# Two rings of PSUM banks in the first layer's attention: from four and three banks to five and two

## The chip, the cores and the metric

The kernel runs on one core of one Trainium2 chip. Five engines work side by side: TensorE (PE) multiplies and writes PSUM alone, VectorE (DVE) and ScalarE (ACT) read PSUM, GpSimd (POOL) works in SBUF, and SyncE (SP) issues transfers. PSUM has eight banks of 128 x 512 float32 here. The metric is the time of one execution in microseconds (us) on the device, the median of several runs.

## The reference, cut to what matters

Two layers over a batch of eight sequences of 512 tokens with 128 channels. The change lies in the attention of the first layer (`L0`): 16 heads of 8 channels, keys within 256 positions of the query.

```python
q, k, v = (proj(w, b) for w, b in ((wq, bq), (wk, bk), (wv, bv)))   # 16 heads of 8
...
scores = jnp.einsum('bhncd,bhnkd->bhnck', qb, kb) / scale
...
scores = jnp.where(valid[None, None], scores, -jnp.inf)
p = jax.nn.softmax(scores, axis=-1)
o = jnp.einsum('bhnck,bhnkd->bhncd', p, vb)
o = o.reshape(B, H, T, D).transpose(0, 2, 1, 3).reshape(B, T, E)
return o @ wo + bo
```

Behind it come a mixture of experts on the same normalised input and the whole second layer, which the change does not touch.

## The kernel before

The first layer's attention takes about the first 525 us. It runs once per sequence (`b`), as a "body" of 64 steps written out one by one: `start` and `first` for sequence 0, six bodies of kind `loop`, then `last`, and `finish`, which holds only the tail of sequence 7. The 64 steps are 4 groups of heads (g) x 4 tiles of 128 queries x 4 heads. Every engine walks through the same steps in this fixed order, and semaphores alone hold one engine back for another; no scheduler moves anything.

Scores are computed twice. In step n PE's `score_rows(n)` multiplies queries by keys into one bank ("rows", 384 or 512 columns), and DVE's `maximum` (L1510) reads it and finds each query's largest score. From the maxima of a group `max_rows` makes `q_max` (L1524). Then `score_cols` computes the scores transposed, with the maximum taken off ("cols"), 21 steps later than the rows of the same number, and ACT's `exp_of` (L1238) writes their exponentials to SBUF. POOL masks them (L1012). Every fourth step ends with `values`, four matmuls of exponentials by values (two passes each, x8 in the trace), into the bank `gather_a`, which belongs to no ring.

So a step of PE is: rows(n), sometimes one thing more, cols(n-21), sometimes one thing more, and in steps with n % 4 = 1 `values`. The things more, per group of 16 steps (n mod 16): at 2 `turn_max` (transposes for `q_max`), at 3 and 7 `select("k")` and `select("q")` of a later group of heads, at 12 `turn_out` (transposes of `o_raw`, which ACT copies out of `gather_a` at L1246). Once per body: `project_v` at step 26, `turn_heads` at 32, `project_out` ("attended") at 36, `turn_x` at 40, `project_raw` at 43 and 45, and the router's logits at 47.

Two rings of banks lie between PE and its readers. A `Fills` object numbers what is filled in the order of the program, puts fill m into slot m modulo the ring's length, and has PE wait, before fill m, until fill m minus the length has been read (`fillable`). Ring M (PE to DVE) takes rows, the transposes of `turn_max`, `turn_out`, `turn_heads`, v, logits and attended: 76 fills in a loop body, in four banks: the three `ring_d` and `gather`. Ring A (PE to ACT) takes cols, `select`, `turn_x` and `project_raw`: 75 fills in a loop body, in three banks: both halves of `ring_a0` and the first half of `ring_a1`. The other half of `ring_a1` is `gather_a`. In the trace, PE's matmuls have the line L458 (L462 for transposes), that of the helper which issues them, and tiles lose their numbers: `ring_a<-q_max,rows` is a cols, `ring_a<-halves,sel` a select, `ring_d<-rows,q_rows` or `gather<-rows,q_rows` a rows, `ring_a<-arena,v_aug` a values.

PE's instructions are issued in order: one that waits for a bank holds up all that stand behind it.

Of the kernel before, what the change touches and what calls it, by code (L numbers as in the profile page):

```python
# [26 lines left out]
B = 8  # L27
T = 512
# [77 lines left out]
class Signal:  # L106


    def __init__(self, ctx, nc, phase, name, per):
        self.name = f"{phase}_{name}"  # L110
        self.sem = ctx.enter_context(nc.semaphore(self.name))
        self.most = 0
        self.per, self.credit, self.n = per, CREDITED.get(name, 0), 0
# [16 lines left out]
class Count:  # L130
# [6 lines left out]
    def open(self, kind, b):  # L137

        assert self.n in (0, self.total), (self.name, kind, self.n, self.total)
        start, first, loop, last, _ = (self.totals[k] for k in BODIES)  # L140
        done = start + first
        self.step, self.known = (b, done - loop) if kind == "loop" else (None, {
            "start": 0, "first": start, "last": done + (B - 2) * loop, "finish": done + (B - 2) * loop + last}[kind])
        self.total, self.n = self.totals[kind], 0
        self.first_fill = {"start": 0, "first": start, "loop": done, "last": done + (B - 2) * loop,
                           "finish": done + (B - 2) * loop + last}[kind]

    def add(self, k):
# [28 lines left out]
class Fills:  # L177


    def __init__(self, body, full, free, slots):  # L180
        self.body, self.full, self.free, self.slots = body, full, free, slots
        self.numbers = {k: {} for k in BODIES}
        assert full.totals["loop"] % len(slots) == 0

    def of(self, what):

# [20 lines left out]
def at_least(eng, count, value):  # L207

    if not isinstance(value, int) or value > 0:
        eng.wait_ge(count.sem, value)  # L210
# [31 lines left out]
def two_layers(nc, x, wq, bq, wk, bk, wv, bv, wo, bo, w_router, w1, b1, w2, b2,  # L242
# [4 lines left out]
    with ExitStack() as ctx:  # L247
        def sb(name, shape, dt=F32):
            return ctx.enter_context(nc.sbuf_tensor(name, shape, dt))
# [5 lines left out]
        banks_d = [ctx.enter_context(nc.psum_tensor(f"ring_d{n}", [P, T], F32)) for n in range(DR)]  # L255
        gather = ctx.enter_context(nc.psum_tensor("gather", [P, T], F32))
        banks_a = [ctx.enter_context(nc.psum_tensor(f"ring_a{n}", [P, 2 * T], F32)) for n in range(AR)]
# [32 lines left out]
        slots, slots_now = sb("slots", [P, TT], U32), sb("slots_now", [P, NT], U32)  # L290
# [8 lines left out]
        full, hi = fulls[:, 0, :], halves[:, 0, :]  # L299
# [95 lines left out]
        def signals(phase, per):  # L395
# [8 lines left out]
            s["D"] = Ring(s["d_full"], s["d_free"], banks_d)  # L404
            s["A"] = Ring(s["a_full"], s["a_free"], banks_a)
            return s

        SA = {name: Count(ctx, nc, name, totals) for name, totals in PER_A.items()}
        now = Body(list(SA.values()))
        M = Fills(now, SA["m_full"], SA["m_free"], [bank[:] for bank in banks_d] + [gather[:]])  # L410
        A = Fills(now, SA["a_full"], SA["a_free"], [banks_a[0][:, 0:T], banks_a[0][:, T:2 * T], banks_a[1][:, 0:T]])
        gather_a = banks_a[1][:, T:2 * T]
        k_dma = [sem(f"k_padded{g}") for g in range(G)]

# [39 lines left out]
        def _(pe):  # L454
            pe.wait_ge(s_pool, N_POOL)

            def mm(out, lhs, rhs, start=True, stop=True):
                return pe.matmul(out, lhs, rhs, start=start, stop=stop, skip_group_check=True)  # L458

            def turn(slot, tile_of, n=NT):  # L460

                return [pe.transpose(slot[:, i * P:(i + 1) * P], tile_of(i), ident[:]) for i in range(n)][-1]  # L462
# [4 lines left out]
            def turn_x():  # L467

                at_least(pe, SA["xn"], SA["xn"].at(1))
                at_least(pe, A.free, A.fillable("xn.T"))  # L470
                turn(A.slot("xn.T"), lambda i: xn[:, i, :]).then_inc(A.full.sem, A.full.add(1))

            def project_raw(which):

                at_least(pe, A.free, A.emptied("xn.T"))
                at_least(pe, A.free, A.fillable(("raw", which)))
                mm(A.slot(("raw", which)), w_nat[:, "kq".index(which), :], xn_t[:]).then_inc(A.full.sem, A.full.add(1))

# [11 lines left out]
            def project_v():  # L490

                at_least(pe, M.free, M.fillable("v"))
                [mm(M.slot("v")[:, i * P:(i + 1) * P], xn_t[:, i * P:(i + 1) * P], wv_sb[:])
                 for i in range(NT)][-1].then_inc(M.full.sem, M.full.add(1))

            def route():

                at_least(pe, M.free, M.fillable("logits"))
                [mm(M.slot("logits")[:, i * NE:(i + 1) * NE], xn_t[:, i * P:(i + 1) * P], router_sb[:])
                 for i in range(NT)][-1].then_inc(M.full.sem, M.full.add(1))  # L500

# [1465 lines left out]
```

## Time and profile before

| what | us |
|---|---|
| median of three runs (1407.49 to 1410.2) | 1408.0 |
| the profiled execution | 1407.57 |
| its span, first to last instruction | 1405.6 |
| PE busy in the span | 1227.9 |
| DVE busy | 902.2 |
| ACT busy | 680.2 |
| POOL busy | 455.8 |
| length of the stage that the change touches, about | 525 |

The profiled execution's own time is 2.0 us above its span; what is added to the span is added to the time. The granted PE clock, in tenths of full speed, is given for slices or stretches of the span.

### The profile page before, as it was taken

How to read it: one execution, taken by the hardware profiler on the slowest of the kernel's cores; microseconds unless marked ns; L12 is line 12 of the kernel's file. 1: busy time of each engine (PE TensorE's matmuls, PEld its weight loads, DVE VectorE, ACT ScalarE, POOL GpSimd, SP SyncE). 2: the span in 40 equal slices, each digit the busy share in tenths (PEclk: the TensorE clock that was granted, in tenths of full speed). 3: DMA queues.
4: the chain of work that ended last, by engine and by line, in shares of the span. 5: the costliest groups of instructions: out<-in, count | busy, mean ns of one | idle time of the engine just before them, and what ended most of it. 6: DMA issues, size and time to landing. Idle time of an engine off the chain costs nothing.

```text
span 1405.6 us, 27026 instructions
## 1 busy us (share of the span) xinstructions
PE 1227.9 (87%) x8812; PEld 844.3 (60%) x8812; DVE 902.2 (64%) x2473; ACT 680.2 (48%) x1293; POOL 455.8 (32%) x694
## 2 busy tenths in 40 slices
PE   3699999999999984999379899898998989989896
PEld 2455556555555543999355656656665576655664
DVE  5788878788888846444345665647565566655744
ACT  1366666766666651444154353553526445254450
POOL 2122212222221216432135253442525335253330
PEclk9899999999999995999679999999999999999999
DMA  2400100100000006112000000000000000000000
GB/s 57 95 17 16 24 16 16 24 16 20 20 16 16 23 2 202 49 45 41 15 5 5 3 12 0 11 4 7 7 0 15 0 7 7 0 15 0 8 2 8
DMA packets 34597, 29.78 MB, mean 21 GB/s; under 512 B 5984, under 2 KB 27104, under 8 KB 34528
## 3 DMA queue, kind: packets, MB, share of 16 engines
q1 hardware_dynamic: 32224, 24.22, 6.5%
q0 software_dynamic: 2304, 4.72, 1.5%
q8 instruction: 34, 0.56, 0.2%
q14 instruction: 35, 0.29, 0.1%
HBM read 13.72 MB, written 6.82 MB: 15 GB/s over the span
## 4 chain that ended last, share of the span: by engine, by line
PE 33%; issue 9%; ACT 5%; DVE 2%; POOL 2%; POOLq 0%; ACTq 0%; DVEq 0%
PE ring_a L458 12%; PE ring_d L458 11%; PE gather L458 7%; ACT arena L1382 3%; PE ring_a L462 2%; ACT xn_all L1362 1%; POOL q_len L1147 1%; DVE arena L1888 0%; POOL klen L1153 0%; DVE k_rows L1816 0%; ACT arena L1354 0%; ACT k_rows L1321 0%; DVE m_cols L1874 0%; POOL arena L1171 0%; DVE q_rn L1752 0%
## 5 line engine op out<-in xcount | busy, mean ns | idle before, releaser
L1238 ACT ACTIVATE arena<-ring_a 128x384 f32<-128x384 f32 (+1 forms) x512 | 255.2, 549 | 152.0 <-PE ring_a L458 152.0
L1382 ACT ACTIVATE arena<-ring_a 128x896 f32<-128x896 f32 (+1 forms) x192 | 163.3, 885 | 205.4 <-PE ring_a L458 205.4
L1510 DVE CUSTOM_DVE_ANT_0 arena<-ring_d,arena 128x384 bf16<-128x384 f32 (+1 forms) x377 | 226.6, 619 | 45.1 <-PE ring_d L458 39.6
L458 PE MATMUL ring_a<-rows,k_rows 64*128 64x512 f32 (+3 forms) x1536 | 159.3, 341 | 43.8 <-ACT xn_all L1362 26.4
L458 PE MATMUL ring_a<-q_max,rows 128*128 128x384 f32 (+1 forms) x512 | 194.5, 383 | 1.0 <-ACT arena L1238 0.5
L1012 POOL TENSOR_SCALAR_AFFINE_SELECT arena<-arena 128x512 f32<-128x512 f32 x128 | 81.9, 640 | 349.5 <-ACT arena L1238 349.5
L458 PEld LDWEIGHTS ring_a<-rows,k_rows 64*128 64x128 f32 x1536 | 119.9, 191 | 81.2 <-ACT xn_all L1362 29.3
L458 PE MATMUL ring_d<-rows,q_rows 128*128 128x384 f32 (+1 forms) x377 | 152.7, 407 | 14.3 <-DMA rows<-k_rows 13.7
L1147 POOL TENSOR_TENSOR q_len<-q_sum,exponents 128x8 f32<-128x8 f32 x64 | 105.2, 1643 | 180.4 <-DVE q_sum L1792 180.4
L458 PE MATMUL ring_d<-arena,v_aug 128*64 128x512 f32 (+3 forms) x1024 | 150.2, 438 | 0.0
L458 PEld LDWEIGHTS ring_d<-rows,q_rows 128*128 128x128 f32 x377 | 72.0, 191 | 92.1 <-DVE mx L1510 43.8
L458 PE MATMUL ring_a<-arena,v_aug 128*32 128x384 f32 (+1 forms) x1024 | 122.8, 551 | 1.0 <-POOL arena L1012 1.0
L458 PEld LDWEIGHTS ring_d<-arena,v_aug 128*64 128x64 f32 x1024 | 68.0, 136 | 78.9 <-issue 68.9
L1171 POOL TENSOR_SCALAR_AFFINE_SELECT arena<-arena 128x256 f32<-128x256 f32 x256 | 97.3, 409 | 42.9 <-ACT arena L1382 42.9
L1792 DVE TENSOR_REDUCE q_sum<-arena 128x8 f32<-128x512 f32 x64 | 43.8, 684 | 100.7 <-ACT arena L1354 100.7
L1510 DVE CUSTOM_DVE_ANT_0 arena<-gather,arena 128x512 bf16<-128x512 f32 (+1 forms) x135 | 84.4, 625 | 34.9 <-PE gather L458 30.0
L458 PEld LDWEIGHTS ring_a<-q_max,rows 128*128 128x128 f32 x512 | 96.0, 188 | 16.5 <-ACT arena L1238 4.5
L1294 ACT ACTIVATE arena<-ring_a,arena 128x128 f32<-128x128 f32 x160 | 50.0, 364 | 75.2 <-PE ring_a L458 75.2
L1846 DVE COPY arena<-ring_d 128x512 f32<-128x512 f32 x64 | 43.8, 685 | 64.8 <-PE ring_d L458 64.8
L1810 DVE TENSOR_TENSOR rows<-arena,rows 128x512 fp32r<-128x512 f32 x64 | 44.6, 697 | 61.9 <-ACT rows L1370 61.0
L458 PE MATMUL ring_a<-arena 128*128 128x128 f32 x320 | 78.1, 399 | 0.0
L458 PEld LDWEIGHTS ring_a<-arena 128*128 128x128 f32 x320 | 76.2, 328 | 0.1
(217 smaller groups left out, 2053.0 us busy)
## 6 DMA issues: line engine op xcount, KB each, us to landing
rows<-k_rows SPq DMA_DIRECT2D x128, 64.0 KB, 2.0
arena<-in_w SPq DMA_DIRECT2D x2, 2048.0 KB, 14.5
slots_y<-arena SPq DMA_DIRECT2D x40, 64.0 KB, 1.6
x_all<-in_x SPq DMA_DIRECT2D x8, 256.0 KB, 4.4
tokens_x<-xn_all SPq DMA_DIRECT2D x1, 2048.0 KB, 9.6
out<-o_t SPq DMA_DIRECT2D x8, 256.0 KB, 2.3
arena<-tokens_x,tokens_now POOLq DMA_INDIRECT x40, 2.6
wq_sb<-in_wq_t SPq DMA_DIRECT2D x1, 512.0 KB, 6.6
```

The source lines that it names most:

```text
L458: return pe.matmul(out, lhs, rhs, start=start, stop=stop, skip_group_check=True)
L462: return [pe.transpose(slot[:, i * P:(i + 1) * P], tile_of(i), ident[:]) for i in range(n)][-1]
L1012: pool.affine_select(out=v, in_=v, compare_op=ALU.is_ge, fill=0.0, base=0, pattern=[[0, HG], [1 if late else -1, P]], channel_multiplier=- ...
L1147: pool.tensor_tensor(q_len[:, 0:2 * NT], q_sum[:, 0:2 * NT], exponents[:, NT:3 * NT], ALU.pow).then_inc(s["lens"].sem, s["lens"].add(1))
L1171: ins = pool.affine_select(out=v, in_=v, compare_op=ALU.is_ge, fill=0.0, base=0, pattern=[[0, 2], [1, P]], channel_multiplier=-1)
L1238: act.activation(probs[:, t % NT, h, 0:many], A.slot(("cols", c))[:, 0:many], ACT.Exp).then_inc(A.free.sem, A.free.add(1))
L1294: ins = act.activation(hidden[:, u % 2, c], hidden_bank(u, c), ACT.Relu, bias=staged[:, u, AT_B1 + c:AT_B1 + c + 1])
L1382: act.activation(dst, src, ACT.Exp).then_inc(A.free.sem, A.free.add(1))
L1510: dve.tensor_tensor_reduce(dump[:, h % 2, 0:many], M.slot(("max", n))[:, 0:many], masks[:, m, at:at + many], 1.0, LOWEST, ALU.add, ALU.max ...
L1792: dve.reduce_sum(q_sum[:, 0:2 * NT], q_sq, AX.X).then_inc(s["sums"].sem, s["sums"].add(1))
L1810: dve.tensor_tensor(q_lo[:, n % QB, :], q_full, q_hi[:, n % QB, :].bitcast(F32), ALU.subtract).then_inc(s["q_lo"].sem, s["q_lo"].add(1))
L1846: dve.tensor_copy(o1[:, n, :], D.slot(("o", n))[:]).then_inc(D.free.sem, D.free.add(1))
```

## The change

One bank, the first half of `ring_a1`, moves from ring A to ring M. Ring A has two places instead of three, ring M five instead of four. Since 76 and 75 are not multiples of 5 and 2, the number of the first fill of a loop body now depends on the body, and the assertion that the rings divide the counts goes. No instruction that computes is added, removed or put elsewhere in the order; banks and the numbers that PE waits for change.

```diff
@@ -142,7 +142,7 @@
         self.total, self.n = self.totals[kind], 0
-        self.first_fill = {"start": 0, "first": start, "loop": done, "last": done + (B - 2) * loop,
+        self.first_fill = {"start": 0, "first": start, "loop": done + (b - 1) * loop, "last": done + (B - 2) * loop,
                            "finish": done + (B - 2) * loop + last}[kind]
@@ -180,7 +180,6 @@
         self.numbers = {k: {} for k in BODIES}
-        assert full.totals["loop"] % len(slots) == 0
@@ -407,8 +406,8 @@
-        M = Fills(now, SA["m_full"], SA["m_free"], [bank[:] for bank in banks_d] + [gather[:]])
-        A = Fills(now, SA["a_full"], SA["a_free"], [banks_a[0][:, 0:T], banks_a[0][:, T:2 * T], banks_a[1][:, 0:T]])
+        M = Fills(now, SA["m_full"], SA["m_free"], [bank[:] for bank in banks_d] + [gather[:], banks_a[1][:, 0:T]])
+        A = Fills(now, SA["a_full"], SA["a_free"], [banks_a[0][:, 0:T], banks_a[0][:, T:2 * T]])
```

Two places on PE, each in the same loop body. The first is steps 2 to 5 of a group, from `turn_max` on: cols, rows, cols, select k, rows, cols, rows, cols, values. The names are out<-in with bank numbers; `ring_a0` stands for either of its two halves; `A_a_free` counts what ACT has read. Before:

```order
L462 MATMUL gather<-ident,m_cols 128x128 x3
L458 MATMUL ring_a0<-q_max,rows 128x384 [waits A_a_free]
L458 MATMUL ring_d0<-rows,q_rows 128x384 [waits A_m_free]
L458 MATMUL ring_a1<-q_max,rows 128x384 [waits A_a_free]
L458 MATMUL ring_a0<-halves,sel 128x512 [waits A_a_free]
L458 MATMUL ring_a0<-halves,sel 128x512
L458 MATMUL ring_d1<-rows,q_rows 128x512 [waits A_m_free]
L458 MATMUL ring_a0<-q_max,rows 128x384 [waits A_a_free]
L458 MATMUL ring_d2<-rows,q_rows 128x512 [waits A_m_free]
L458 MATMUL ring_a1<-q_max,rows 128x512 [waits A_a_free,A_m_free]
L458 MATMUL ring_a1<-arena,v_aug 32x384 [waits A_masked]
```

And now:

```order
L461 MATMUL ring_d2<-ident,m_cols 128x128 x3
L457 MATMUL ring_a0<-q_max,rows 128x384 [waits A_a_free]
L457 MATMUL gather<-rows,q_rows 128x384 [waits A_m_free]
L457 MATMUL ring_a0<-q_max,rows 128x384 [waits A_a_free]
L457 MATMUL ring_a0<-halves,sel 128x512 [waits A_a_free]
L457 MATMUL ring_a0<-halves,sel 128x512
L457 MATMUL ring_a1<-rows,q_rows 128x512 [waits A_m_free]
L457 MATMUL ring_a0<-q_max,rows 128x384 [waits A_a_free]
L457 MATMUL ring_d0<-rows,q_rows 128x512 [waits A_m_free]
L457 MATMUL ring_a0<-q_max,rows 128x512 [waits A_a_free,A_m_free]
L457 MATMUL ring_a1<-arena,v_aug 32x384 [waits A_masked]
```

The order is the same. All five fills of ring A now share the two halves of `ring_a0`: the select takes the bank of the cols two fills before it, and the last cols that of the select. `ring_a1` takes a rows.

The second place is steps 6 to 9 of the same group, around select q. Before:

```order
L458 MATMUL gather<-rows,q_rows 128x512 [waits A_m_free]
L458 MATMUL ring_a0<-q_max,rows 128x512 [waits A_a_free]
L458 MATMUL ring_d0<-rows,q_rows 128x512 [waits A_m_free]
L458 MATMUL ring_a0<-q_max,rows 128x512 [waits A_a_free]
L458 MATMUL ring_a1<-halves,sel 128x512 [waits A_a_free]
L458 MATMUL ring_a1<-halves,sel 128x512
L458 MATMUL ring_d1<-rows,q_rows 128x512 [waits A_m_free]
```

And now:

```order
L457 MATMUL ring_d1<-rows,q_rows 128x512 [waits A_m_free]
L457 MATMUL ring_a0<-q_max,rows 128x512 [waits A_a_free]
L457 MATMUL ring_d2<-rows,q_rows 128x512 [waits A_m_free]
L457 MATMUL ring_a0<-q_max,rows 128x512 [waits A_a_free]
L457 MATMUL ring_a0<-halves,sel 128x512 [waits A_a_free]
L457 MATMUL ring_a0<-halves,sel 128x512
L457 MATMUL gather<-rows,q_rows 128x512 [waits A_m_free]
```

Here too only banks differ: the select moved from `ring_a1` to the bank of the cols that stands two fills before it.

## Rows read from the trace of the kernel before

**Rows 1.** The page: span, and busy time of PE and its weight loads.

```profile
span 1405.6 us, 27026 instructions
PE 1227.9 (87%) x8812; PEld 844.3 (60%) x8812; DVE 902.2 (64%) x2473; ACT 680.2 (48%) x1293; POOL 455.8 (32%) x694
```

**Rows 2.** Busy time, in three stretches: PE, PEld, DVE, ACT, POOL, then granted clock, DMA share, GB/s.

```profile
100.00:450.00 350.00, 334.32 (x1984) 203.27 (x1984) 288.96 (x1010) 232.40 (x479) 77.87 (x117) 1.00 0.08 18
...
530.00:560.00 30.00, 11.89 (x44) 10.00 (x45) 19.96 (x43) 2.38 (x5) 22.64 (x46) 0.50 0.77 236
...
900.00:1000.00 100.00, 91.61 (x796) 62.00 (x796) 61.54 (x130) 45.87 (x71) 46.22 (x66) 1.00 0.03 7
```

**Rows 3.** Groups by line and shape, 100 to 450 us: exponentials, both widths.

```profile
L1238 ACT ACTIVATE arena<-ring_a 128x512 f32<-128x512 f32 x188 | 109.1, 606 | 48.9 <-PE ring_a L458 48.9
...
L1238 ACT ACTIVATE arena<-ring_a 128x384 f32<-128x384 f32 x185 | 82.7, 492 | 65.6 <-PE ring_a L458 65.6
```

**Rows 4.** Waits, 100 to 450 us: total us, times, longest us.

```profile
PEld ring_d L458 <- DVE mx L1510: 30.9, 48, 0.8
...
PEld ring_d L462 <- ACT o_raw L1246: 18.0, 24, 0.9
...
PEld ring_a L458 <- ACT halves L1211: 4.1, 6, 0.7
...
PEld ring_a L458 <- DVE q_max L1524: 2.3, 6, 0.4
```

**Rows 5.** Timeline, one group of 16 steps, 270.81 to 284.20 us.

```profile
271.47 1.64 ACT L1238 ACTIVATE arena<-ring_a 128x384 f32<-128x384 f32 x4 [0.92 <-PE ring_a L458]
...
271.62 0.19 PEld L458 LDWEIGHTS ring_a<-q_max,rows 128*128 128x128 f32 x1
...
272.01 0.19 PEld L458 LDWEIGHTS ring_a<-q_max,rows 128*128 128x128 f32 x1
...
272.41 1.06 PE L458 MATMUL ring_a<-arena,v_aug 128*32 128x512 f32 x8
...
273.41 0.19 PEld L458 LDWEIGHTS ring_d<-rows,q_rows 128*128 128x128 f32 x1 [0.84 <-DVE mx L1510]
...
274.48 0.36 PEld L458 LDWEIGHTS ring_a<-halves,sel 128*128 128x128 f32 x2
274.50 0.87 ACT L1238 ACTIVATE arena<-ring_a 128x384 f32<-128x384 f32 x2 [1.39 <-PE ring_a L458]
...
274.65 0.62 PE L458 MATMUL ring_a<-halves,sel 128*128 128x512 f32 x2
...
275.32 0.69 ACT L1220 ACTIVATE k_rows<-ring_a,ones_row 128x512 fp32r<-128x512 f32 x1
...
275.52 0.19 PEld L458 LDWEIGHTS ring_a<-q_max,rows 128*128 128x128 f32 x1
...
276.07 0.85 PE L458 MATMUL ring_a<-arena,v_aug 128*32 128x384 f32 x8
...
276.86 0.19 PEld L458 LDWEIGHTS gather<-rows,q_rows 128*128 128x128 f32 x1 [0.62 <-DVE mx L1510]
...
277.62 1.09 ACT L1238 ACTIVATE arena<-ring_a 128x512 f32<-128x512 f32 x2 [0.75 <-PE ring_a L458]
...
277.66 0.42 PEld L458 LDWEIGHTS ring_a<-halves,sel 128*128 128x128 f32 x2
...
278.59 0.61 ACT L1222 ACTIVATE q_rows<-ring_a 128x512 fp32r<-128x512 f32 x1
...
278.81 0.19 PEld L458 LDWEIGHTS ring_a<-q_max,rows 128*128 128x128 f32 x1
...
279.35 0.16 PEld L458 LDWEIGHTS ring_a<-arena,v_aug 128*32 128x32 f32 x8 [0.35 <-issue]
...
282.04 0.42 PEld L462 LDWEIGHTS ring_d<-ident,o_raw 128*128 128x128 f32 x4 [0.92 <-ACT o_raw L1246]
...
284.20 0.19 PEld L458 LDWEIGHTS ring_d<-rows,q_rows 128*128 128x128 f32 x1 [0.84 <-DVE mx L1510]
```

## The prediction

> **What bounds the kernel now.** I first read the page: PE is busy 1227.9 of 1405.6 us, DVE 902.2 and ACT 680.2 [rows 1]. That is a mean over stages, so I cut out the stage of the change. From 100 to 450 us PE is busy 334.32 of 350 us, DVE 288.96, ACT 232.40, and the clock is granted in full, 1.00 [rows 2]. A row of PE is to be read with care, because its matmuls overlap, so I then asked what PE waits for. The table of waits names DVE first: 30.9 us over 48 waits [rows 4]. It would follow that ring M is too short. The timeline says otherwise. The weight load of the rows behind a `values` always stands 0.84 us "behind DVE" when the values had 512 columns and 0.62 us when they had 384 [rows 5]; 30.9/48 is 0.64, a mixture of just these. The load comes 1.00 us after the values' matmuls began (272.41 to 273.41) or 0.79 us (276.07 to 276.86), never at another distance. That is the length of the values' own streaming, 1.06 and 0.85 us busy with the drain in it; DVE merely happened to be the last to have signalled. PE works there. The real waits of PE are few: for `o_raw`, 18.0 us over 24 times; for the second raw projection, 4.1 over 6; for `q_max`, 2.3 over 6 [rows 4].
>
> So PE, in order, sets the pace, and it waits neither for DVE nor, but for the six, for ACT. What a loop body costs: cols are 188 + 185 = 373 in 350 us [rows 3], 0.938 us a step, 60.0 us for 64 steps.
>
> **Ring M, four to five.** What a fifth bank can take away is a wait of PE for DVE to read a rows. After the correction above no such wait of weight is left, and I price this part at 0. Bound on the side of a gain: if all of the 30.9 us in 350 were true, then over some 480 us of bodies 30.9/350 x 480 = 42 us. I take 0, because the gaps have the two fixed lengths of the streaming, not lengths that vary with DVE. A rule reads such rows the other way: the Trainium skill, "Perfetto Trace Analysis", section "Optimization Strategy", says that a gap which repeats on the engine that should be saturated can mean too few PSUM buffers. By it the repeated gap would be worth up to those 42 us; by the row it is worth nothing. A bank's new reader costs nothing: DVE reads as many columns as before.
>
> **Ring A, three to two.** Now fill m waits for the reading of fill m-2 and not m-3. I re-time one plain group [rows 5], 270.81 to 284.20 us. I need two small figures. With three banks the fourth of four narrow cols had just to wait for the first: the four exponentials start at 271.47 and one takes 0.492 us [rows 3], which ends at 271.96, and the load came at 272.01. So from the end of the reading to PE's weight load 0.05 us pass. And a load normally leads its matmul (274.48 to 274.65, 0.17 us), while after a wait the lead is shorter; I take the matmul's delay as the load's less 0.1 us.
>
> - *Four narrow cols (steps 14 to 1).* The third one's load stood at 271.62; it must now wait for the first exponential, to 272.01: +0.39. The four exponentials take 1.64 us, so the second ends (1.64 - 0.49)/3 = 0.38 us after the first, at 272.34, and the fourth load comes at 272.39 instead of 272.01: +0.38, not additive. All that follows is 0.38 us later.
> - *Around select k (steps 2 to 5).* Its load (274.48) waits for the first exponential (274.50 + 0.49 = 274.99), to 275.04: +0.56; matmuls +0.46. Its matmuls ended at 275.27 and now at 275.73; ACT's copy of 0.69 us, which began at 275.32, begins at 275.78 and ends at 276.47. The last cols needs that bank: 276.52 instead of 275.52, +1.00, less 0.1: +0.90.
> - *Around select q (steps 6 to 9).* The first exponential ends 277.62 + 0.61 = 278.23; the select's load moves from 277.66 to 278.28, matmuls +0.52; the copy from 278.59 to 279.11, ending at 279.72; the last cols' load from 278.81 to 279.77, +0.96, less 0.1: +0.86.
> - *Steps 10 to 13.* 0: here `turn_out` waits 0.92 us for `o_raw` anyway, and no cols stands within two fills of an unread one. That wait is no reserve for the others, since `o_raw` hangs on the values before it and moves with them.
>
> A group: 0.38 + 0.90 + 0.86 = 2.14 us; four: 8.6. Of that three things go once per body. The `q_max` wait (2.3/6 = 0.4) already holds the last cols of one group: -0.4. `turn_heads` stands between narrow cols and gives ACT the time: -0.4. `project_out` stands between select k and the last cols, likewise, and has a wait for DVE of its own: -0.9. Three more fills of ring A enter, x transposed and two raw projections, each read by ACT in 0.6 to 1.3 us; one of them waits 0.7 us already [rows 4]. I take +0.75, an estimate between 0 and three times the 0.56 of a select (1.7). Sum: 8.6 - 1.7 + 0.75 = 7.6 us per loop body (rounded), 60.0 to 67.6.
>
> Behind PE everything shifts as a whole: ACT's and DVE's work per body is unchanged, and both had waited for PE (48.9 + 65.6 us before the exponentials alone [rows 3]).
>
> All bodies: six loop bodies 45.6. `first` has cols in 43 of 64 steps: 43/64 x 7.6 = 5.1. `last` has no next sequence, so no raw projections and no selects of group 0: 5. `finish` has 21 cols, mostly held by ACT already: 1.5. Sum 57.2 us. On the profiled execution's 1407.57 us that is **1465 us**; its median of three, 1408.0, lies 0.4 us higher, which is inside the rounding.
>
> **Rivals.**
>
> - *The fifth bank pays (faster).* The mechanism is the table of waits taken at its word: PE does wait for DVE's maximum before the rows that follow values. Place: the 48 waits; price: up to -42 us, 1366 us before what ring A costs. It decides if ring A's waits come to under 42 us. For it: the table and ACT's busy share of 232.40 in 350. Against: the two fixed lengths. Chance 4%.
> - *Nothing moves.* ACT is a third idle, and the waits at ring A fall into places where PE would have waited for something else. Then 1408 us. For it only the means speak; in the re-timed group all but one of the places have no other wait. Chance 3%.
> - *Half the price.* The waits for `o_raw`, 24 of 0.75 us, are after all a reserve (if ACT takes its exponentials earlier relative to values). 2.14 - 0.75 = 1.39 a group, 5.6 for four, less 1.7 plus 0.75 gives 4.6 per body; counted as 7.5 bodies (57.2/7.6) 35 us: 1442 us. Chance 15%.
> - *Nothing is absorbed.* 8.6 + 1.7 = 10.3 us per body, 77 us in all: 1485 us. Chance 13%.
> - *The clock falls.* Where PE was busy only 11.89 of 30 us its granted clock was 0.50, the lower of the two levels; at 91.61 of 100 us it was 1.00 [rows 2]. After the change PE would be busy about 57 of 67.6 us, 85%, nearer to the second. If it fell for a tenth of PE's time, that tenth would take twice as long: 5.7 us per body, 43 in all on top: 1508 us. Chance 4%. The Trainium skill, "TensorE: Matmul & The Clock Gate", section "A second HAM failure mode: psum-queue depth-cycling", tells of a kernel in which short idles between groups, from cycling through PSUM banks, made the clock swing; no stretch of this trace with PE over nine tenths busy shows that.
>
> **How the numbers follow.** The forecast itself, within 1450 to 1479, has 61%. The range reaches down to the half price, 1440, and up to the case without absorption, 1485, and leaves out the rest. A measurement of this kernel tells 0.2%, about 3 us, from no change. Slower by more: 0.61 + 0.15 + 0.13 + 0.04 = 0.93; same 0.03; faster 0.04.
>
> **What would show it.** In the profile after: (1) a row "PEld ring_a <- ACT arena L1237" among the longest waits, some 12 per body, where none stands now, and "<- ACT k_rows" and "q_rows" before the last cols of two stretches per group; (2) the gaps of 0.84 and 0.62 us behind `values` as before, whether named DVE or "issue", which proves the first paragraph; (3) 67 to 68 us per body; (4) DVE waiting longer for PE; (5) clock 1.00 in the stage; (6) nothing different behind it. The prediction is wrong if the gaps behind values shrink, if ACT's copies of the selects come no later against the loads, or if PE's rows can be seen issued past a waiting cols.

## The result and the profile after

The changed kernel takes 1469.64 us (median of four runs, 1466.49 to 1471.78) against 1407.74 us before: 1.0436 times as long, 95% interval 1.0408 to 1.0463. Forecast were 1465 us, 1440 to 1485. The profiled execution took 1467.64 us, 60.1 more than the 1407.57 of before; the sum had said 57.2.

The page of the changed kernel: span, busy times, and the granted clock in 40 slices of the span.

```profile
span 1465.7 us, 27027 instructions
...
PE 1268.2 (87%) x8812; PEld 841.3 (57%) x8812; DVE 902.1 (62%) x2473; ACT 696.0 (47%) x1293; POOL 457.0 (31%) x694
...
PEclk9899999999999999599958999999999999999998
```

DVE's work is the same to 0.1 us. PE "works" 40.3 us more though it runs the same 8812 matmuls. Their records overlap: where nothing waits, a narrow matmul's record lasts 0.34 us and the next begins 0.17 us after it (271.27 and 271.44 in the trace of before). When the next one is held up, more of the record before it counts as busy, and the one behind the wait is itself about 0.1 us longer, 0.44 us at 297.70 in the rows below. How the 40.3 us divide between the two was not worked out. The share of busy time, 87%, has not moved at all, which shows how little it tells about a kernel that got 4% slower.

Where the time lies is told by the issue of the transfer `tokens_x`, the first thing behind the stage. Before and after:

```profile
L922 SPq DMA_DIRECT2D tokens_x<-xn_all x1: 391/391/391, 529.2 to 529.2; - x1
```

```profile
L921 SPq DMA_DIRECT2D tokens_x<-xn_all x1: 392/392/392, 587.4 to 587.4; - x1
```

587.4 - 529.2 = 58.2 us of the 60.1 stand in the first layer's attention.

Busy time and clock of the changed kernel from 100 to 450 us (PE, PEld, DVE, ACT, POOL, clock), which answers to the first of [rows 2], and the waits of the same stretch, which answer to [rows 4]:

```profile
100.00:450.00 350.00, 321.89 (x1758) 176.36 (x1754) 255.55 (x892) 216.50 (x425) 69.54 (x105) 1.00 0.07 17
```

```profile
PEld ring_a L457 <- ACT arena L1237: 30.8, 62, 0.7
PEld ring_d L457 <- DVE mx L1509: 30.7, 42, 0.8
...
PEld gather L457 <- DVE mx L1509: 11.7, 16, 0.8
PEld ring_a L457 <- DVE mx L1509: 11.5, 16, 0.8
...
PEld ring_a L457 <- ACT q_rows L1221: 6.8, 16, 0.4
...
PE ring_a L457 <- ACT k_rows L1219: 3.5, 15, 0.2
```

The first row is new: 62 waits of PE for an exponential, where [rows 4] had none. The rows that name DVE are still there, now split over the bank names `ring_d`, `gather` and `ring_a`, because rows rotate through five banks: 42 + 16 + 16 = 74 waits of at most 0.8 us. Before, they were 71 and not 48, since the table of before has a second row of this kind, for `gather`. It has a third row with DVE in it, a short one, in which matmuls stand still and not only weight loads:

```profile
PEld gather L458 <- DVE mx L1510: 17.2, 23, 0.9
...
PE gather L458 <- DVE mx L1510: 3.5, 6, 0.6
```

This last row, once per body, has no counterpart in the changed kernel. It is the one wait that the fifth bank did take away, as the section on the experiments shows; the gaps behind `values` it did not touch. The clock stayed at 1.00, its upper level.

The order of the weight loads in a plain group of 16 steps, with ACT's instructions that hold them up (start, length, engine; the idle time before each in brackets). It answers to [rows 5]:

```profile
296.50 0.19 PEld L457 LDWEIGHTS gather<-rows,q_rows 128*128 128x128 f32 x1 [0.84 <-DVE mx L1509]
...
297.16 1.90 ACT L1237 ACTIVATE arena<-ring_a 128x384 f32<-128x384 f32 x4 [0.92 <-PE ring_a L457]
297.70 0.19 PEld L457 LDWEIGHTS ring_a<-q_max,rows 128*128 128x128 f32 x1 [0.36 <-ACT arena L1237]
297.70 0.44 PE L457 MATMUL ring_a<-q_max,rows 128*128 128x384 f32 x1
...
298.46 1.06 PE L457 MATMUL ring_a<-arena,v_aug 128*32 128x512 f32 x8
...
300.55 0.87 ACT L1237 ACTIVATE arena<-ring_a 128x384 f32<-128x384 f32 x2 [1.49 <-PE ring_a L457]
301.09 0.30 PEld L457 LDWEIGHTS ring_a<-halves,sel 128*128 128x128 f32 x2 [0.55 <-ACT arena L1237]
...
301.85 0.69 ACT L1219 ACTIVATE k_rows<-ring_a,ones_row 128x512 fp32r<-128x512 f32 x1 [0.43 <-PE ring_a L457]
...
302.65 0.19 PEld L457 LDWEIGHTS ring_a<-q_max,rows 128*128 128x128 f32 x1 [0.58 <-issue]
...
303.08 0.85 PE L457 MATMUL ring_a<-arena,v_aug 128*32 128x384 f32 x8
...
305.27 0.30 PEld L457 LDWEIGHTS ring_a<-halves,sel 128*128 128x128 f32 x2 [0.66 <-ACT arena L1237]
...
306.70 0.19 PEld L457 LDWEIGHTS ring_a<-q_max,rows 128*128 128x128 f32 x1 [0.43 <-ACT q_rows L1221]
...
307.13 0.85 PE L457 MATMUL ring_a<-arena,v_aug 128*32 128x384 f32 x8
...
309.82 0.42 PEld L461 LDWEIGHTS ring_a<-ident,o_raw 128*128 128x128 f32 x4 [0.92 <-ACT o_raw L1245]
...
311.99 0.19 PEld L457 LDWEIGHTS ring_d<-rows,q_rows 128*128 128x128 f32 x1 [0.84 <-DVE mx L1509]
```

Each stretch runs from one `values` to the next (the first and last from the rows behind one):

| stretch | before | after | more | forecast |
|---|---|---|---|---|
| four narrow cols | 270.81 to 272.41: 1.60 | 296.50 to 298.46: 1.96 | 0.36 | 0.38 |
| around select k | 272.41 to 276.07: 3.66 | 298.46 to 303.08: 4.62 | 0.96 | 0.90 |
| around select q | 276.07 to 279.35: 3.28 | 303.08 to 307.13: 4.05 | 0.77 | 0.86 |
| steps 10 to 13 | 279.35 to 284.20: 4.85 | 307.13 to 311.99: 4.86 | 0.01 | 0 |
| group | 13.39 | 15.49 | 2.10 | 2.14 |

The load at 302.65 shows how to read a releaser: it says "issue" (elsewhere DVE), but k_rows ends at 301.85 + 0.69 = 302.54 and its matmul's own row says `[0.23 <-ACT k_rows L1219]`. It is the select's bank that the cols waits for.

### The profile page after: what moved, and what is told of

It is laid out like the page before. It is cut to its first block, busy times and chain, and to the rows that moved or that the text cites. A ratio compares the mean times of both kernels' runs of the same rounds, so it can differ in the third digit from the quotient of the medians.

```text
span 1465.7 us, 27027 instructions
## 1 busy us (share of the span) xinstructions
PE 1268.2 (87%) x8812; PEld 841.3 (57%) x8812; DVE 902.1 (62%) x2473; ACT 696.0 (47%) x1293; POOL 457.0 (31%) x694
## 4 chain that ended last, share of the span: by engine, by line
PE 69%; issue 12%; ACT 11%; POOL 3%; DVE 3%; SPq 1%; DMA 1%; POOLq 0%; ACTq 0%; DVEq 0%
PE ring_a L457 38%; PE ring_d L457 17%; PE gather L457 9%; ACT arena L1237 3%; PE ring_a L461 3%; ACT arena L1381 3%; PE ring_d L461 1%; ACT xn_all L1361 1%; ACT k_rows L1219 1%; ACT o_raw L1245 1%; POOL v_aug L1040 1%; POOL q_len L1146 1%; PE gather L461 1%; DVE rows L1585 0%; SPq L876 0%
## 5 line engine op out<-in xcount | busy, mean ns | idle before, releaser
L1237 ACT ACTIVATE arena<-ring_a 128x384 f32<-128x384 f32 (+1 forms) x512 | 263.7, 542 | 170.5 <-PE ring_a L457 164.4
L1509 DVE CUSTOM_DVE_ANT_0 arena<-ring_d,arena 128x384 bf16<-128x384 f32 (+1 forms) x312 | 187.5, 621 | 86.8 <-PE ring_d L457 84.5
L457 PE MATMUL ring_a<-q_max,rows 128*128 128x384 f32 (+1 forms) x512 | 205.5, 403 | 11.6 <-ACT k_rows L1219 5.2
L457 PE MATMUL ring_d<-rows,q_rows 128*128 128x384 f32 (+1 forms) x312 | 125.0, 403 | 12.7 <-DMA rows<-k_rows 12.4
L457 PEld LDWEIGHTS ring_d<-rows,q_rows 128*128 128x128 f32 x312 | 59.7, 192 | 74.3 <-DVE mx L1509 48.0
L1509 DVE CUSTOM_DVE_ANT_0 arena<-gather,arena 128x512 bf16<-128x512 f32 (+1 forms) x100 | 62.1, 621 | 25.9 <-PE gather L457 25.3
L457 PE MATMUL gather<-wout_sb,arena 128*128 128x128 f32 x512 | 68.8, 281 | 8.7 <-DVE arena L1887 8.7
```

Of the source, the lines that this page charges most:

```text
L1237: act.activation(probs[:, t % NT, h, 0:many], A.slot(("cols", c))[:, 0:many], ACT.Exp).then_inc(A.free.sem, A.free.add(1))
L1509: dve.tensor_tensor_reduce(dump[:, h % 2, 0:many], M.slot(("max", n))[:, 0:many], masks[:, m, at:at + many], 1.0, LOWEST, ALU.add, ALU.max ...
```

## The experiments

Each is compared with the kernel before, run on the same chip. `e1` to `e3` change the lists of banks alone, `e4` also gives the selects a ring with semaphores of its own. Beside the time of the whole kernel stands the length of a loop body, from one router projection to the next in the kernel's trace. Within a trace the six loop bodies mostly agree to 0.03 us, so it can tell what the times of whole executions, which scatter by several us, cannot. It is the length in one execution of each kernel: 59.9 us before (one body 60.15), 67.8 in the changed kernel.

**e1: only ring A's loss.**

```diff
-        M = Fills(..., [bank[:] for bank in banks_d] + [gather[:], banks_a[1][:, 0:T]])
+        M = Fills(..., [bank[:] for bank in banks_d] + [gather[:]])
```

> Ring A two banks as in the change, ring M four as before; the eighth bank is used by nobody. Theory (only ring A's lost bank costs, ring M was never short): the time of the changed kernel, 1466 to 1473 us. Rival (the fifth bank of ring M earns part of the 42 us that the table of waits offers, and ring A costs more than is seen): slower than the changed kernel by over 3 us, 1473 to 1510 us.

Measured: 1470.02 us, ratio 1.044 (1.0412 to 1.0469). The changed kernel's own ratio is 1.0436. Taking the fifth bank away again costs nothing that these intervals, some 4 us wide to each side, can tell, and a bank worth 42 us is excluded.

The traces are finer, and there ring M was short in one place. The six loop bodies of e1 take 68.3 to 68.4 us, those of the changed kernel 67.8. All of the difference, 0.53 us, lies in the one stretch between two `values` that holds `project_out`: 5.56 us in e1, 5.03 with the fifth bank; every other stretch agrees to 0.02 us. The kernel before shows why:

```profile
239.94 0.34 PE L458 MATMUL gather<-rows,q_rows 128*128 128x384 f32 x1
...
242.50 0.55 DVE L1510 CUSTOM_DVE_ANT_0 arena<-gather,arena 128x384 bf16<-128x384 f32 x1
...
242.98 0.08 DVE L1510 DVE_READ_ACCUMULATOR2_ANT mx<- 128x1 f32 x1
...
243.21 0.57 PE L458 MATMUL gather<-arena,o_t 128*128 128x128 f32 x3 [0.59 <-DVE mx L1510]
```

The bank `gather` is filled by a rows. Four fills later `attended` wants the same bank, but DVE, which has meanwhile copied `o_t` and normalised x, reads the rows only from 242.50 to 243.06. So PE stands still for 0.59 us: the bank's old content had not yet been read. In e1 the same wait is 0.3 us (5 times in 350 us), and in the changed kernel `attended` follows the matmul before it with no wait. Over some 7.5 bodies the fifth bank is worth about 4 us: a tenth of the rival's 42, but not the 0 of the theory.

**e2: ring M with three, ring A with three.**

```diff
+        M = Fills(..., [bank[:] for bank in banks_d[:2]] + [gather[:]])
+        A = Fills(..., [banks_a[0][:, 0:T], banks_a[0][:, T:2 * T], banks_a[1][:, 0:T]])
```

> Ring A three banks as before, ring M three; one bank unused. Theory (with four banks PE never waits for DVE): with three, by the group of rows 5, the fourth narrow rows waits for the maximum three before it, some 0.4 us per group and a little more where DVE has other work: 2 to 3 us per body, 1420 to 1430 us. Rival (the waits for DVE behind values are true): each of the eight or so per body grows by one maximum, 0.55 to 0.7 us, at least 5 us per body: 1445 us or more.

Measured: 1419.27 us, ratio 1.0077 (1.005 to 1.0104), 11 to 12 us more than before, just below the range that was said (1420 to 1430) and far from the rival's 1445. A body takes 61.5 us, 1.5 more than before, where 2 to 3 were expected. The table of waits of this kernel (100 to 450 us):

```profile
PEld ring_d L457 <- DVE mx L1509: 46.1, 80, 0.8
PEld gather L457 <- DVE mx L1509: 22.4, 39, 0.8
```

119 waits against 71 before, in which true short ones are now mixed with the streaming, and with gaps that the table of before put down to "issue" or to other instructions of DVE. At three banks the ring bites in most groups: the stretch with the narrow cols is 0.24 us longer. At four it bites once per body, at `attended`.

**e3: the change turned round, four for ring A, three for ring M.**

```diff
+        M = Fills(..., [bank[:] for bank in banks_d[:2]] + [gather[:]])
+        A = Fills(..., [banks_a[0][:, 0:T], banks_a[0][:, T:2 * T], banks_a[1][:, 0:T], banks_d[2][:]])
```

> The change turned round: ring A four banks, ring M three. Theory: ring A was short only at the second raw projection (0.7 us per body) and by 0.05 us at the fourth narrow cols, so this is 5 to 8 us below the kernel with three and three, 1413 to 1424 us, and not faster than before. Rival (any bank given to ring A pays as much as the one taken from it cost): 1350 to 1400 us.

Measured: 1413.79 us, ratio 1.0044 (1.0029 to 1.0058). 5.5 us below the kernel with three and three and still above before, as expected. The two intervals overlap a little, but no run of either kernel falls among those of the other, and a body takes 60.8 us instead of 61.5, nearly all of it in the stretch with the second raw projection (4.81 instead of 5.45 us). So for ring A the third bank is worth 62 us, and a fourth one, beside three for ring M, 5.5.

**e4: the selects in a bank of their own.** Ring A has two banks, ring M four, and the eighth bank is a ring S of length one, with its own semaphores.

```diff
+        S = Fills(now, SA["s_full"], SA["s_free"], [banks_a[1][:, 0:T]])
...
-                at_least(pe, A.free, A.fillable(("sel", which, g)))
+                at_least(pe, S.free, S.fillable(("sel", which, g)))
```

> Ring A two banks, but the two select fills of a group go to the eighth bank, a ring of one of their own; ring M four. Theory (most of the cost is the select, which waits for an exponential and whose copy holds the bank of the last cols): 0.90 and 0.86 us of each group go, 0.38 for narrow cols and about 0.75 per body for raw projections and the transposed x stay: 1.9 us per body, 1422 us, 1417 to 1430. Rival (two banks are too few for the cols and their exponentials as such): over 1445 us.

Measured: 1426.37 us, ratio 1.0143 (1.0097 to 1.0189). Two banks nearly carry the cols and their exponentials; 43 of the 62 us, give or take 8, hang on the selects, which push into the same ring. A body takes 61.9 us, 5.9 less than in the changed kernel and 1.9 to 2.0 more than before; 1.9 was expected. The narrow cols still wait, as the weight loads of this kernel show, and around select k nothing waits any more:

```profile
291.02 0.19 PEld L459 LDWEIGHTS ring_a<-q_max,rows 128*128 128x128 f32 x1 [0.38 <-ACT arena L1239]
...
293.84 0.36 PEld L459 LDWEIGHTS ring_a<-halves,sel 128*128 128x128 f32 x2
...
294.88 0.19 PEld L459 LDWEIGHTS ring_a<-q_max,rows 128*128 128x128 f32 x1
```

**e5: less work for DVE.** Do the gaps of 0.84 and 0.62 us behind `values` depend on DVE? The banks are those of before; every maximum reads half its columns, the other half being left out of it.

```diff
-                dve.tensor_tensor_reduce(dump[:, h % 2, 0:many], M.slot(("max", n))[:, 0:many], masks[:, m, at:at + many],
+                dve.tensor_tensor_reduce(dump[:, h % 2, 0:many // 2], M.slot(("max", n))[:, 0:many // 2], masks[:, m, at:at + many // 2],
```

> The kernel before with its four and three banks, but every maximum on DVE reads only the first half of its bank's columns (192 or 256); the second half is left out of the maxima, so this is no attention any more, and only its time is read. DVE's 64 maxima per body get shorter by some 0.2 to 0.27 us each, 13 to 17 us per body. Theory (PE does not wait for DVE at ring M): the gaps of 0.84 and 0.62 us behind values stay as they are; only the waits for q_max, for the heads and for the attended go, at most 1.5 us per body: 1396 to 1407 us. Rival (the table of waits is true): up to 42 us faster, 1366 to 1390 us.

Measured: 1399.99 us, ratio 0.9952 (0.9934 to 0.9971). Busy time and waits of this kernel, 100 to 450 us, and two of its weight loads behind `values`:

```profile
100.00:450.00 350.00, 337.95 (x2018) 206.16 (x2016) 218.18 (x1024) 234.56 (x485) 77.80 (x118) 1.00 0.08 18
```

```profile
PEld ring_d L458 <- DVE mx L1510: 48.9, 66, 0.8
...
PEld gather L458 <- DVE mx L1510: 14.2, 23, 0.8
```

```profile
202.79 0.19 PEld L458 LDWEIGHTS ring_d<-rows,q_rows 128*128 128x128 f32 x1 [0.63 <-DVE mx L1510]
...
206.87 0.19 PEld L458 LDWEIGHTS ring_d<-rows,q_rows 128*128 128x128 f32 x1 [0.84 <-DVE mx L1510]
```

DVE is busy 218.18 us instead of 288.96, and yet the largest row that has PE waiting for DVE has grown, from 30.9 us over 48 waits to 48.9 over 66. The growth itself is a matter of names: gaps that the table of before puts down to `o_t`, `o_n` or "issue" now have the name of the maximum. All gaps before weight loads of the line L458 into `ring_d` and `gather` together are 74.8 us over 106 in the table of before and 73.3 us over 107 here. So with a quarter less work for DVE the gaps are as many and as long as they were. They kept their two lengths, and DVE is not their cause. That they are the streaming of the `values` is argued from those lengths.

What was won, 7 us, lies in two places of the body, which takes 59.2 us instead of 59.9: 0.26 us in the stretch with the wait for `q_max` and 0.50 us in that of `attended`, whose wait for the bank is gone. The heads' transposes gave nothing.

**e6, e7, e8: the wait for `o_raw`.** Three kernels move `turn_out` and `divide`, which hang on one constant, to later steps.

```diff
-AT_TURN_MAX, AT_TURN_OUT, AT_OUT_ROWS, AT_SEL_K, AT_SEL_Q = 18, 44, 42, 51, 55
+AT_TURN_MAX, AT_TURN_OUT, AT_OUT_ROWS, AT_SEL_K, AT_SEL_Q = 18, 45, 42, 51, 55
```

> The kernel before, with turn_out and divide one step later (45 instead of 44 in each group of 16), so that another rows and cols stand between ACT's copy of o_raw and its transposes. Theory (the wait of 0.92 us before turn_out is the largest true wait of PE that is left, of which 0.5 us are empty time on PE): 0.3 to 0.45 us less per group, 1.2 to 1.8 us per body, 1394 to 1400 us. Rival (the wait just moves to the cols or the values behind it): 1405 to 1410 us.

Measured: 1397.84 us, ratio 0.9944 (0.9923 to 0.9965), 9.3 us faster than before. A body takes 58.8 us, 1.15 less, just under the 1.2 to 1.8 that were expected. In steps 10 to 13 lay time that no ring decides.

> The changed kernel with turn_out one step later. Theory (steps 10 to 13 cost nothing with two banks since turn_out's wait for o_raw stood there, and the exponentials had been read by then): without that wait the last two cols of the stretch come earlier and may have to wait for their bank, so less is won than with three banks: 1460 to 1469 us. Rival (the wait for o_raw has nothing to do with ring A): as much is won as with three banks, 9 to 13 us, 1456 to 1460 us.

Measured: 1462.23 us, ratio 1.0384 (1.0361 to 1.0407), 7.4 us less than the changed kernel against 9.3 with three banks. The value lies in the theory's range and outside the rival's, but the two gains differ by 1.9 us only, less than the intervals can separate. The bodies separate them: one step later takes 0.9 us off each with two banks (66.9 instead of 67.8) and 1.15 with three. The waits for exponentials did rise, from 62 to 84 places and from 30.8 to 39.5 us in 350:

```profile
PEld ring_a L457 <- ACT arena L1237: 39.5, 84, 0.7
```

So the exponentials did move into the gap and took about 0.25 us of the gain per body, some 2 us in all, as the theory has it.

> The kernel before with turn_out and divide two steps later (46 instead of 44). Theory: one step later the weight load still waited for o_raw in 18 places from 100 to 450 us, up to 0.6 us, of which matmuls stood still for about 0.2 us; a second step takes that too: 1 to 4 us less than one step later, 1393 to 1397 us. Rival (one step later was already enough, or the later transposes hold up the heads' transposes at step 32): the time of one step later or more, 1397 to 1402 us.

Measured, with 46 in place of 44: 1407.19 us beside 1405.98 for before on that chip, ratio 1.0002 (0.9983 to 1.0021). Nothing is left of the gain that these runs can tell, and the theory falls; the value lies above the rival's range too. The waits for `o_raw` are gone from this kernel's table, but these stand there (350 us):

```profile
PEld ring_d L462 <- DVE o_n L1533: 6.4, 6, 1.1
...
PEld ring_a L458 <- ACT halves L1211: 6.1, 6, 1.0
```

The heads' transposes now wait for `divide`, and the second raw projection waits longer (4.1 us in [rows 4]). Once per body each; together some 8 us more in 350. That these two rows account for all of the lost gain was not tested. The trace is of the shortest of the twelve executions, 1400.85 us, and its bodies take 59.4 to 60.5 us, about as long as before and 0.6 us or more longer than with one step.

## Why the prediction was right

**What bounds.** PE in order, and DVE in one place only: e5 shows it (a quarter less work for DVE, the same gaps), and e1 bounds the fifth bank. What the Trainium skill, "Perfetto Trace Analysis", section "Optimization Strategy", names as a possibility for gaps that repeat did not apply to those behind `values`; they stayed with five banks. For ring A after the change it does: there the repeated gaps before select and cols are a missing bank.

**What the prediction missed.** Its reading of the table of waits took in `ring_d` alone. With the 17.2 us of `gather` its bound on the fifth bank's gain would have been 66 us and not 42. And "no such wait of weight is left" passed over 3.5 us of standing matmuls, the wait of `attended` for its bank: the price of 0 for ring M should have been a gain of 0.53 us per body, about 4 us. It did give `project_out` "a wait for DVE of its own", but as something that absorbs a delay of ring A and not as what the fifth bank takes away.

**The group.** 2.10 us against 2.14, and each stretch within 0.1 us. The three mechanisms are seen in the rows: the third narrow cols waits 0.36 for the first exponential; the select waits 0.55 and 0.66 for one; the copy then holds the bank of the last cols for 0.58 and 0.43. e4 took the selects out of the ring and with them 43 us. By the stretches (0.96 + 0.77) x 4 x 7.5 is 52 us; less where `project_out` and the `q_max` wait already cover it, that is the right size.

**Once per body.** The body after, from one router projection to the one two bodies later:

```profile
212.66 1.03 PEld L457 LDWEIGHTS ring_d<-router_sb,xn_t 128*128 128x128 f32 x8
...
348.29 1.03 PEld L457 LDWEIGHTS ring_d<-router_sb,xn_t 128*128 128x128 f32 x8
```

(348.29 - 212.66)/2 = 67.8 us; forecast 67.6, before 60.0. The terms inside moved a little against each other. The `values` loads around the transposed x, the two raw projections, the router and the next select k, of before and then of after:

```profile
245.78 0.16 PEld L458 LDWEIGHTS ring_a<-arena,v_aug 128*32 128x32 f32 x8 [0.36 <-issue]
...
249.59 0.16 PEld L458 LDWEIGHTS ring_a<-arena,v_aug 128*32 128x32 f32 x8 [0.36 <-issue]
...
255.03 0.16 PEld L458 LDWEIGHTS ring_a<-arena,v_aug 128*32 128x32 f32 x8 [0.76 <-issue]
...
258.51 0.16 PEld L458 LDWEIGHTS ring_a<-arena,v_aug 128*32 128x32 f32 x8 [0.25 <-issue]
...
262.66 0.16 PEld L458 LDWEIGHTS ring_a<-arena,v_aug 128*32 128x32 f32 x8 [0.24 <-issue]
```

```profile
267.94 0.16 PEld L457 LDWEIGHTS ring_a<-arena,v_aug 128*32 128x32 f32 x8 [0.24 <-issue]
...
272.68 0.16 PEld L457 LDWEIGHTS ring_a<-arena,v_aug 128*32 128x32 f32 x8 [0.37 <-issue]
...
279.02 0.16 PEld L457 LDWEIGHTS ring_a<-arena,v_aug 128*32 128x32 f32 x8 [0.76 <-POOL arena L1011]
...
282.83 0.16 PEld L457 LDWEIGHTS ring_a<-arena,v_aug 128*32 128x32 f32 x8 [0.19 <-issue]
...
287.52 0.16 PEld L457 LDWEIGHTS ring_a<-arena,v_aug 128*32 128x32 f32 x8 [0.24 <-issue]
```

The four stretches take 4.74, 6.34, 3.81 and 4.69 us instead of 3.81, 5.44, 3.48 and 4.15: +0.93, +0.90, +0.33, +0.54. The last one needs care: this is the body of 60.15 us, and in the five others of before that stretch takes 3.93 us and not 4.15, so that it grows by 0.77. Two further stretches hold the heads (3.05 before, 3.36 after) and `attended` (5.40 and 5.03). Against plain stretches the terms come out so, in us per body:

| term | forecast | measured |
|---|---|---|
| four plain groups | +8.6 | +8.4 |
| transposed x and raw projections | +0.75 | +1.07 |
| `q_max` wait absorbs | -0.4 | -0.2 |
| heads absorb | -0.4 | -0.05 |
| `project_out` absorbs | -0.9 | -0.8 |
| fifth bank of ring M | 0 | -0.53 |
| sum | +7.6 | +7.9 |

The group, nearly all of the sum, was right in its mechanism and its size. That the sum came as close as 0.3 us is in part luck: the raw projections and the absorptions were each off by 0.1 to 0.35 us on one side, the fifth bank by 0.53 us and the four groups by 0.2 us on the other. The sum as a whole fell 2.9 us short of the profiled execution: 1.0 us inside the stage (58.2 against 57.2) and 1.9 us behind it, where nothing was changed and the runs scatter by as much.

**The rivals.** "The fifth bank pays" fell at its price with e1 and e5; some 4 us of it are true. "Nothing moves" fell with the result. "Half the price" rested on the wait for `o_raw` as a reserve: steps 10 to 13 kept it whole (0.92 us in both traces), because the copy moves with the values. "Nothing is absorbed" fell too: 1.05 of the 1.7 us per body were absorbed. "The clock falls" did not happen: 1.00 from 100 to 450 us. There PE was busy 321.89 of 350 us, 92% and not the 85% that this rival reckoned with. The failure that the Trainium skill, "TensorE: Matmul & The Clock Gate", section "A second HAM failure mode: psum-queue depth-cycling", describes is not seen in the stage in these runs, although PE stops some 12 times per body for an exponential and a further six times or so for a select's copy.

## What to carry to other kernels

A ring's length is to be judged by the burst that passes through it, and by the slowest thing in the burst: two banks served cols and exponentials at a cost of 2 us per body, and cost 8 when a select with its copy entered the same ring. Before giving a ring another bank, look whether the waits that name its reader have varying lengths; waits of one or two fixed lengths may be the streaming of what stands before, which a run with less work for the reader can tell. Look also at the rows of matmuls that stand still, however short: one wait per body for a bank hid among the false ones. And a wait is no reserve if what it waits for moves with the delay.

## What was not expected of the hardware

A weight load behind the eight passes of `values` comes 1.00 or 0.79 us after they began, and no earlier when DVE had far less to do (e5) or a bank more stood free; for one and the same gap the profile names now DVE, now "issue". And moving `turn_out` and `divide` by one step paid 9.3 us, by two steps nothing that the runs can tell (e6, e8).
